# A residual attention and MLP block on one core: both halves of the last six x turns go into two PSUM banks, and the body opens in another order

## What is computed

```
xn  = layernorm(x)
s   = xn @ Win + bin                          # 64 numbers for each row
h   = relu(s[..., None] * W1 + b1)            # 64 x 16
g   = sum over the 16 of (h * W2) + b2        # 64 numbers
out = x + attention(xn) + (g @ Wout + bout)
```

## Time and profile before

| | |
|---|---|
| time, median of 3 runs | 326.89 us (325.35 to 327.45) |
| the profiled execution's own time | 325.13 us |
| its span, first to last instruction | 323.4 us |
| TensorE busy | 294.6 us, 91% |
| VectorE busy | 253.3 us, 78% |
| GpSimd busy | 236.5 us, 73% |
| ScalarE busy | 234.2 us, 72% |
| granted TensorE clock, mean | 0.995 |
| DMA | 87.80 MB, mean 272 GB/s |

### The profile page before, as it was taken

The page is one execution under the profiler, slowest core; times in us unless marked ns, Lnnn a source line. Parts: engine busy times, 40 slices in busy tenths (PEclk is TensorE's granted clock), DMA queues, the critical chain, the costliest instruction groups (busy, mean ns, idle before and its releaser), DMA issues.

```text
span 323.4 us, 5159 instructions
## 1 busy us (share of the span) xinstructions
PE 294.6 (91%) x1804; PEld 129.9 (40%) x1804; DVE 253.3 (78%) x400; ACT 234.2 (72%) x308; POOL 236.5 (73%) x209
## 2 busy tenths in 40 slices
PE   3788879988989999999999999999999999998892
PEld 3644635444424544344353434343333343432220
DVE  1648559579599787996789999999897989995445
ACT  1528654875797869879798668888878788888840
POOL 8530899932984989559891966978969597989950
PEclk9999999999999999999999999999999999999998
DMA  7999939995639799698979999899999998333597
GB/s 240 304 373 404 263 28 335 403 271 148 195 117 337 211 343 295 197 350 228 339 188 321 314 299 317 237 358 260 327 324 341 350 368 284 132 131 155 206 286 280
DMA packets 50569, 87.80 MB, mean 272 GB/s; under 512 B 6360, under 2 KB 35184, under 8 KB 46448
## 3 DMA queue, kind: packets, MB, share of 16 engines
q1 hardware_dynamic: 46400, 65.96, 67.0%
q10 hardware_dynamic: 3504, 21.37, 18.3%
q0 software_dynamic: 640, 0.16, 0.8%
HBM read 53.77 MB, written 33.69 MB: 270 GB/s over the span
## 4 chain that ended last, share of the span: by engine, by line
PE 41%; DVE 22%; DMA 15%; SPq 10%; issue 7%; ACT 2%; POOL 2%; ACTq 0%; DVEq 0%
DMA xq<-in_L_attn_x_dram 12%; PE op L568 10%; PE g L536 9%; PE s L490 7%; DVE x L989 6%; DVE stats L1016 6%; SPq L237 4%; SPq L256 4%; PE TA L466 4%; DMA out_dram<-x 3%; PE rep L520 2%; DVE xqT L999 2%; DVE SL L1010 1%; SPq L259 1%; ACT H L746 1%
## 5 line engine op out<-in xcount | busy, mean ns | idle before, releaser
L1134 POOL TENSOR_TENSOR x<-x,bias_row 128x512 f32<-128x512 f32 x128 | 162.6, 1308 | 0.0
L746 ACT ACTIVATE H<-rep,b1c,w1c 128x1024 f32<-128x1024 f32 x124 | 142.4, 1221 | 14.1 <-PE rep L520 12.2
L989 DVE TENSOR_TENSOR x<-x,op 128x1024 f32<-128x1024 f32 x59 | 71.4, 1210 | 25.9 <-PE op L568 25.9
L1016 DVE BATCH_NORM_STATS2 stats<-x 128x6 f32<-128x512 f32 x128 | 80.8, 678 | 8.4 <-DMA x<-in_L_attn_x_dram 8.4
L568 PE MATMUL op<-wout,G 64*128 64x512 f32 x236 | 65.0, 627 | 3.7 <-DVE x L989 2.9
L1118 POOL TENSOR_TENSOR rstd<-veps,nhalf 128x8 f32<-128x8 f32 x16 | 26.7, 1670 | 50.5 <-DVE veps L1026 50.5
L536 PE MATMUL g<-H,w2s 128*32 128x512 f32 x512 | 63.4, 600 | 0.0
L490 PE MATMUL s<-xT,win 128*64 128x512 f32 x128 | 59.9, 612 | 1.6 <-ACT xqT L720 1.6
L720 ACT ACTIVATE xT<-TA 128x512 f32<-128x512 f32 x64 | 38.5, 605 | 25.2 <-PE TA L466 21.2
L466 PE MATMUL TA<-ident,x 128*128 128x128 f32 x288 | 47.8, 299 | 5.2 <-DMA x<-in_L_attn_x_dram 3.0
L490 PE MATMUL s<-xqT,winq 128*64 128x512 f32 x112 | 51.1, 599 | 0.0
(11 more groups left out here) (174 smaller groups left out, 284.2 us busy)
## 6 DMA issues: line engine op xcount, KB each, us to landing
out_dram<-x SPq DMA_DIRECT2D x30, 1024.0 KB, 6.2
x<-in_L_attn_x_dram ACTq DMA_DIRECT2D x10, 2048.0 KB, 11.7
xq<-in_L_attn_x_dram SPq DMA_DIRECT2D x112, 128.0 KB, 7.6
x<-in_L_attn_x_dram SPq DMA_DIRECT2D x12, 1024.0 KB, 11.9
out_dram<-x SPq DMA_DIRECT2D x4, 512.0 KB, 3.3
x<-in_L_attn_Wq_dram SPq DMA_DIRECT2D x1, 1024.0 KB, 17.4
x<-in_L_attn_Wk_dram SPq DMA_DIRECT2D x1, 1024.0 KB, 19.6
x<-in_L_attn_Wv_dram SPq DMA_DIRECT2D x1, 1024.0 KB, 16.0
```

Source lines behind the costliest of these rows:

```text
L746: act.activation(Hr[half][k % len(Hr[half])][:, :], rep_banks(n, half)[:, :], ACT.Relu, bias=b1c[:, half, k:k + 1], scale=w1c[:, half, k:k ...
L989: dve.tensor_tensor(both, both, sum_banks(n, j)[:, :].rearrange("p (h d) -> p h d", h=2), ALU.add).then_inc(add_done, 1)
L1016: dve.bn_stats(stats[:, j, :], x_sb[m][:, j * D:(j + 1) * D]).then_inc(bn_done, 1)
L1134: pool.tensor_tensor(x_sb[m][:, c], x_sb[m][:, c], bias_row[:, :], ALU.add).then_inc(xc_done, 1)
```

## The change

For pairs from 10 on (`TWO = 10`) the groups of x turns alternate between `T_ps` and `A_ps`, so a group waits for the copy of the group before the last, not of the last. In pair 10 itself the second group still waits for the first one's copy and for `att_made`. The bodies of pairs 10 to 15 are written as loops of their own, without `reach`. On TensorE T1 follows T0, `spread_rstd` comes next, ahead of project 0 and of `replicate(n-2, 1)`, and T2 and T3 stand together ahead of `replicate(n-1, 0)`. On ScalarE `evacuate_g(n-2)` moves ahead of `evacuate(n, 2)` and `evacuate(n, 3)`. VectorE, GpSimd and SyncE keep their orders. No instruction's work is added or taken away.

```diff
+        TWO = 10
...
-            return A_ps if n < BY_PE and g % 2 else T_ps
+            return A_ps if (n < BY_PE or n >= TWO) and g % 2 else T_ps
...
-                free = groups(n) + g - (1 if n < BY_PE else 0)
+                free = groups(n) + g - (1 if n < BY_PE or n > TWO or (n == TWO and g > 1) else 0)
+                if n == TWO and g == 1:
+                    pe.wait_ge(att_made, 1)
...
-            for n in range(N):
+            for n in range(TWO):
...
+            for n in range(TWO, N):
+                transpose(n, 0)
+                transpose(n, 1)
+                spread_rstd(n - 1)
+                project(n - 3, 0)
+                replicate(n - 2, 1)
+                project(n - 3, 1)
+                sum_h(n - 2, 0)
+                project(n - 3, 2)
+                sum_h(n - 2, 1)
+                sum_h(n - 2, 2)
+                sum_h(n - 2, 3)
+                transpose(n, 2)
+                transpose(n, 3)
+                replicate(n - 1, 0)
+                project(n - 3, 3)
+                s_product(n)
...
+            for n in range(TWO, N):
+                evacuate(n, 0)
+                relu(n - 2, 4)
+                copy_rstd(n - 1)
+                evacuate(n, 1)
+                relu(n - 2, 5)
+                relu(n - 2, 6)
+                relu(n - 2, 7)
+                s_high(n - 1)
+                if has(n + AHEAD):
+                    load_pair(n + AHEAD)
+                evacuate_g(n - 2)
+                evacuate(n, 2)
+                evacuate(n, 3)
+                for r in range(HK):
+                    relu(n - 1, r)
```

## The result

The changed kernel takes 330.31 us (median, 329.46 to 332.21), the kernel before 327.17 in the same comparison: the ratio is 1.0149, with a 95% interval of 1.0099 to 1.0199. The change makes the kernel slower, by 1.0 to 1.5%: the two medians lie only 3.14 us apart, 1.0%, and the recorded ratio is not their quotient. The profiled execution took 329.85 us with a span of 328.1, both 4.7 more than before, which is 1.5%.

A forecast was written before the change was run, and what follows sets the result against it. TensorE, busy throughout quiet pairs of 15.24 us, was taken as the bound. The terms 6.3 + 0.86 - 1.58 - 0.45 gave +5.1 us on the median of 326.89, so 332.0 us; range 328.8 to 334.5.

The forecast's parts named there:

- the second bank wins: Rival for the whole kernel: the adds stay hidden, -2.8 us in all, 324.1 us; chance 0.07.
- only project 1's wait counts: Rival: handover at its lower bound, project 2's wait absorbed, +2.2 us in all, 329.1 us; chance 0.15.
- Project 1 too early: TensorE, pairs from 10: project 1 waits for VectorE's add of project 0, 2.45 needed against 1.52, +0.93 us a pair.
- Project 2: TensorE, each pair: with T2 gone, steps give 2.05 where the handover wants 2.45, +0.40 us a pair.
- Sum 0 next in line by 0.12: TensorE: sum 0 may start 3.38 us after project 0, behind the 1/std copy, and wants to at 3.50; nothing paid.
- Turns together: TensorE: T2 and T3 as one run save 0.18, T0 before another turn the rest, about 0.27 us a pair.
- Pair 10's entry: TensorE, pair 10: T1 waits for T0's copy, 1.35 us where 0.49 would do, +0.86 once.
- Store waits: Pairs 12 and 13: T3's waits for ScalarE copies behind a store go with two banks, -1.58 us in all.
- The spread and GpSimd: TensorE: the earlier spread waits for GpSimd's wide 1/std, costing nothing, with 0.2 us to spare in the worst pair.
- The tail: After the body: TensorE's idle of 0.54 us for the fourth relu nearly goes, -0.45, bounds 0 and -0.54.
- the half case: Rival: project 1's wait alone is paid, with the handover at its lower bound, +2.2 us, 329.1; chance 0.15.
- The rival of the clock: TensorE: short idles drop the clock to 1.2 GHz for a whole pair, up to 15 us more, above 340; chance 0.02.

The follow-up runs named there:

- old opening: Changed kernel with TensorE's opening put back to T0, project 0, replication, T1, spread, project 1: 325.36 us, ratio 1.0008 to the kernel before.
- turns apart: Changed kernel with T2 moved back between sum 0 and project 2: 331.25 us, ratio 1.0183 to the kernel before.
- second sum: Changed kernel with the old opening, sum 1 ahead of project 2, and ScalarE's sixth relu ahead of the second x copy: 324.57 us, ratio 0.9935 to the kernel before.
- project first: Changed kernel with project 0 moved ahead of T0: 330.69 us, ratio 1.0137 to the kernel before.
- banks only: Kernel before with only the second bank used from pair 10 on, both orders unchanged: 325.19 us, ratio 0.9981 to the kernel before.
- replication in front: Second sum kernel opening with project 0, replication, T0, T1, spread; ScalarE's fifth relu before the first x copy; pair 10's T1 freed from T0's copy: 324.71 us, ratio 0.9941.

## Why the prediction was right

The forecast was 332.0, which is +5.1 us on the kernel before. Measured were 330.31, and +4.7 between the profiled executions; the medians themselves lie 3.14 apart. The mechanism was the one forecast: with projects 2.45 apart, the rivals in which the second bank wins, or only project 1's wait counts, are out. By its steps:

- **Project 1 too early**, +0.93 a pair from a handover of 2.45 read in the tail. The projects stand 2.46 apart and the idle is 0.85. Taken away alone (old opening), the pair falls from 16.26 to 15.48. Shown.
- **Project 2**, +0.40. They stand 2.45 apart, the idle is 0.33; it goes when T2 is put back between (turns apart) and when sum 1 is (second sum). Shown.
- **Sum 0 next in line by 0.12.** In the changed kernel the copy ends at 220.62 and sum 0 starts at 220.81, a slack of 0.19. Once the adds are out of the way, in the order of project first, it waits 1.02 for that copy. Shown; the 0.8 without the adds was made for the changed order, so the two sizes compare only roughly.
- **Turns together**, -0.27 a pair. T0 and T1 take 0.92 for 0.99, T2 and T3 1.03 for 0.99. The pair came out at 16.25 to 16.27 for 16.29.
- **Pair 10's entry**, +0.86: T1 starts 1.44 after T0, not 1.35, and the pair lasts 0.99 longer than pair 11.
- **Store waits**, -1.58. None reaches TensorE here, and pairs 12 and 13 cost 0.33 and 0.29 more than before instead of 1.05. But that the second bank is the cause is not shown in this kernel: its loads of these pairs went out at 239.63 and 256.74, and no idle of ScalarE is put down to a store, so there was no such wait to hide. The kernel with banks only shows the bank's part (1.43 and 1.99 on ScalarE, none on TensorE), and the one with the replication in front its limit.
- **The spread and GpSimd**, 0.2 to spare in the worst pair. Pair 12 lost 0.15 there (16.41 for 16.26): GpSimd's wide 1/std, begun at 232.00, ends 0.97 after the pair's T0 (232.09), and the spread starts at 1.03 for 0.92. The estimate was slightly on the wrong side.
- **The tail**, -0.45 for the fourth relu. From project 3 to the replication 5.14 became 4.75, so -0.39. The body by itself grew by 5.29, for 5.1 forecast.
- **Luck.** Two parts of the 4.7 were not forecast. The stretch behind the body is 0.43 shorter, 0.28 of it a wait for the low part that is gone, and pair 10 begins 0.16 sooner. Without them the step would be 5.3.
- **The median.** The 1.8 us that I added to come from the profiled execution to the median is what puts 332.0 above 330.31; the step itself was +5.1 for +4.7. The kernel before's own execution lay 1.8 below its median and the changed kernel's only 0.5 below.
- **The chances** don't add up as written: 0.63, 0.13 and 0.02 less a tenth come to 0.68 or 0.70, and not 0.76, for slower by over 1%. The range's lower end, 328.8, has no term behind it, since the half case gives 329.1.

The rival of the clock, which the Trainium skill raises (TensorE: Matmul & The Clock Gate, "A second HAM failure mode: psum-queue depth-cycling"), didn't come: the granted clock is 1.00 in every pair, though each has two short idles.

## What to carry to other kernels

When steps are regrouped on a saturated engine, list for every pair of steps that share a buffer how far apart they start, and how long the step and the other engine's answer take together: here a distance of 2.55 us hid a chain of 2.45, and taking 1.0 out of it cost 0.9 a pair. A second buffer only helps the wait that it was made for; the order that it permits must be checked against all other waits. Removing one wait brings up the next (0.19 us behind it here), so an order is to be tried as a whole, with the filler (a sum, a turn) placed where a handover needs it: by the recorded ratios that made the kernel 0.65% faster than before, where the change had made it 1.5% slower.

## What the runs showed that I had not expected

The time of a step on TensorE depends on its neighbour: a projection and a replication, both with 64 rows of weights, take 1.52 us side by side and 1.72 with a 128-row turn between them, with no wait in either case. Two turns side by side save 0.14 (T2 and T3, 1.03 for 1.17) to 0.17 (T0 and T1, 0.92 for 1.09), so an order that brings turns together can lose more than that by parting two such steps. And in three kernels a saving at one place (0.78 in pair 10, 1.58 of store waits, 0.47 at the replication) came back wholly or for the most part as waits for another engine's results within the same or the next pairs.
